# Row means from eight extra columns of a weight matrix, and reciprocal roots spread by two fp32r products, in the last stage of a four-layer kernel

## Chip, core and metric

One core of a Trainium2 chip runs the whole program in one launch. The metric is the device time of that launch in microseconds. TensorE (PE in the profile) multiplies, ScalarE (ACT) and VectorE (DVE) take tiles out of PSUM, GpSimd (POOL) works on SBUF alone, and SyncE (SP) issues nearly all transfers.

## What is computed

The input x is (8, 256, 256) fp32: 2048 tokens of 256 channels. Four residual layers follow each other, cut here to what matters:

```python
x = x + L0(x)      # 3 shared dense layers and 2 of 4 experts per batch, mixed by a gate
x = x + L1(x)      # 8 gated experts (silu(x Wg) * (x Wu)) Wd weighted per batch, and a shared one
def L2(x):         # per batch b a language id picks W1 (256x64), b1, W2 (64x256), b2, gamma, beta
    h = relu(x @ w1 + b1)
    x = x + (h @ w2 + b2)
    mean = x.mean(-1); var = ((x - mean) ** 2).mean(-1)
    return (x - mean) * rsqrt(var + 1e-5) * gamma + beta
x = x + L2(x)
def L3(x):         # per batch b a subject id picks weight (256x256) and bias
    return x @ weight.T + bias
x = x + L3(x)
```

## The kernel before

Channels lie on the partitions, in two halves of 128 (`dt` 0 and 1), and tokens along the free dimension. An fp32 product is made of three fp32r products: each operand is held as a rounded part (`xh`, made by ACT with a Copy) and the rest (`xl`, made by DVE or POOL as a difference), and `product` (L439) adds hi by hi, hi by lo and lo by hi.

**The last stage** works off the ninth expert of layer 1 in five jobs of tokens, `LAST_JOBS` (L39): three of 512 tokens and two of 256. Each job has eight steps T. In a step PE issues the twelve products of `last_up` (L760) for tile T and the six of `last_down` (L780) for tile T - 2; ACT makes the silu (L1387) and the rounded hidden tile (L1395), DVE multiplies (L2243) and takes the difference (L2250). So `last_up(n)` waits for DVE's product of tile n - 2 (`gated_done`), and `last_down(n)` for the difference of tile n (`hid_lo`).

**Layers 2 and 3** of a job ride on the steps of the jobs behind it. The five jobs are the units 0 to 4 of `unit` (L303); the last, 4, is called `END`. The table `WHEN` (L54) gives for each unit and each stage name the step T behind which the stage's instructions stand, on each engine in its own program order. For a unit i they are:

- `last_take` (L2224, DVE) adds job i into x; `x2` makes its parts (ACT L1412, DVE L2279). `xs` sums the two channel halves of x for units 1 and 2 (POOL L1848), and splits the sum (ACT L1455, POOL L1504).
- `up`: `l2_up_stage` (PE, L803), the first matrix of layer 2, 64 rows into PSUM. `mean`: `mean_stage` (PE, L831), products with `minus_mean`, a 128x128 tile filled with -1/256, which leave minus the row mean in every partition: two of 512 columns for units 1 and 2 (L841, L842), two per channel half and part, four in all, for units 0 and 3 (L850, L851). For END `mean_part` (L822) issues eight of 256 columns (L828), four ahead of `x_part(4, 0)` and four behind the wait for the hidden tile.
- `hid` (or `within` for unit 0, inside a step): ACT writes relu of the hidden tile twice, as fp32 and as fp32r (L1445, L1446), once per batch; DVE adds the mean to x (L2291, twice) and writes the difference of the hidden tile into the lower 64 rows of `u` (L2294).
- `down`: `l2_down_stage` (PE, L854), both parts of the second matrix against the 128 rows of `u`. END's `x_part(4, 1)` follows it.
- `res` (DVE, L2308), `square` (ACT L1421, DVE L2317, L2321, POOL L1859), `scale` (ACT, L1431), `var` (PE, L884), `eps` (DVE, L2328), then on POOL the power -1/2 (L1866) and on ACT `diag` (L1462), which scales the 128x128 unit matrix by the reciprocal root, a block of 128 tokens at a time.
- `rstd` (PE, L892): an fp32 product of ones with that diagonal matrix spreads the roots over all partitions. END has no `diag` and no `rstd`.
- `norm` (DVE, L2337), `add` (DVE, L2347), `x3` and `x3l` (ACT L1412, DVE L2279), `l3a` and `l3b` (PE, L908 to L910), `outa` and `outb` (DVE, L2395), and the store (SP, L431).

END ends otherwise: `split` (ACT L1476, DVE L2363), `scaled` (PE, L955 to L957), `base` (DVE, L2373) and `final` (DVE, L2383).

Weights of layers 2 and 3 are loaded late, one batch b per chunk: `w3_plus_one` and `late_lo` (POOL, L1822, L1831), `center_w2` (DVE, L2255) and `late_hi` (ACT, L1397), spread by `late_step` (L299). `b2_stage` (PE, L797) and `center_b2` (DVE, L2266) stand at T = 9.

## Time and profile before

| | us |
|---|---|
| median of 3 runs | 1579.68 |
| their lowest and highest | 1579.55, 1579.96 |
| the profiled execution's own time | 1579.32 |
| its span, first to last instruction | 1577.2 |
| busy share of the span: PE, PE's weight loads, DVE, ACT, POOL | 100%, 85%, 72%, 59%, 43% |
| mean granted clock of TensorE | 0.999 of full speed |

The span is the time between the first and the last instruction of one execution; 2.1 us of that execution lie around it. Starts are counted from the span's start. A row of the timeline gives start, duration, engine, line, operation, the tile written and the tiles read, shapes, a count where equal instructions are merged, and in brackets the idle time ahead of it with the instruction that ended it. Ends of matmuls are modelled: the distance from one start to the next tells more than a duration.

### The profile page before, as it was taken

How to read it: one execution, taken by the hardware profiler on the slowest of the kernel's cores; microseconds unless marked ns; L12 is line 12 of the kernel's file. 1: busy time of each engine (PE TensorE's matmuls, PEld its weight loads, DVE VectorE, ACT ScalarE, POOL GpSimd, SP SyncE). 2: the span in 40 equal slices, each digit the busy share in tenths (PEclk: the TensorE clock that was granted, in tenths of full speed). 3: DMA queues.
4: the chain of work that ended last, by engine and by line, in shares of the span. 5: the costliest groups of instructions: out<-in, count | busy, mean ns of one | idle time of the engine just before them, and what ended most of it. 6: DMA issues, size and time to landing. Idle time of an engine off the chain costs nothing.

```text
span 1577.2 us, 22436 instructions
## 1 busy us (share of the span) xinstructions
PE 1571.8 (100%) x7916; PEld 1341.1 (85%) x7916; DVE 1132.3 (72%) x1685; ACT 930.7 (59%) x1683; POOL 674.7 (43%) x631
## 2 busy tenths in 40 slices
PE   9999999999999999999999999999999999999999
PEld 7888888999988888888888888888888888888898
DVE  6855556688889876776777776776776776657567
ACT  6655555666666665565565566666656666555444
POOL 7865544756786441431432432342342352038000
PEclk9999999999999999999999999999999999999999
DMA  4111105455420000000010010010010010022000
GB/s 161 55 54 53 54 27 187 161 178 181 174 85 27 27 28 27 22 33 27 15 41 28 14 41 27 14 40 28 14 41 27 14 41 27 15 60 77 14 14 28
DMA packets 31013, 85.98 MB, mean 55 GB/s; under 512 B 5031, under 2 KB 10535, under 8 KB 30775
## 3 DMA queue, kind: packets, MB, share of 16 engines
q1 hardware_dynamic: 30310, 83.21, 15.5%
q8 instruction: 63, 1.03, 0.3%
q0 software_dynamic: 304, 1.10, 0.2%
q14 instruction: 48, 0.39, 0.1%
q10 hardware_dynamic: 288, 0.26, 0.1%
HBM read 82.46 MB, written 2.10 MB: 54 GB/s over the span
## 4 chain that ended last, share of the span: by engine, by line
PE 97%; issue 2%; POOL 1%; DMA 0%; ACT 0%; DVE 0%; POOLq 0%; DVEq 0%
PE up L684 13%; PE up L682 13%; PE up L683 13%; PE sum L441 13%; PE sum L443 13%; PE sum L442 13%; PE up L441 4%; PE up L442 4%; PE up L443 4%; PE up L449 2%; PE up L451 2%; PE up L450 2%; POOL expert_in L1504 0%; PE sum L630 0%; DMA raw<-in_shared 0%
## 5 line engine op out<-in xcount | busy, mean ns | idle before, releaser
L1313 ACT ACTIVATE hidden_hi<-up_tile 128x512 fp32r<-128x512 f32 x256 | 161.3, 630 | 189.3 <-DVE up_tile L2155 166.7
L2160 DVE TENSOR_TENSOR hidden_lo<-up_tile,hidden_hi 128x512 fp32r<-128x512 f32 x256 | 197.8, 792 | 44.7 <-ACT hidden_hi L1313 44.7
L2150 DVE TENSOR_TENSOR gate_tile<-up,gate_tile 128x512 f32<-128x512 f32 x192 | 129.9, 687 | 139.1 <-PE up L684 138.5
L443 PE MATMUL sum<-hidden_hi,down 128*128 128x512 f32 x512 | 199.2, 389 | 0.0
L441 PE MATMUL sum<-hidden_hi,down 128*128 128x512 f32 x512 | 199.2, 389 | 0.0
L442 PE MATMUL sum<-hidden_lo,down 128*128 128x512 f32 x512 | 199.2, 389 | 0.0
L684 PE MATMUL up<-x_sums,gate_up 128*128 128x512 f32 x512 | 199.2, 389 | 0.0
L682 PE MATMUL up<-x_sums,gate_up 128*128 128x512 f32 x512 | 199.2, 389 | 0.0
L683 PE MATMUL up<-x_sums,gate_up 128*128 128x512 f32 x512 | 199.2, 389 | 0.0
L2155 DVE TENSOR_TENSOR up_tile<-up_tile,gate_tile 128x512 f32<-128x512 f32 x192 | 183.8, 984 | 2.2
L1306 ACT ACTIVATE gate_tile<-gate_tile 128x512 f32<-128x512 f32 x192 | 119.8, 632 | 90.5 <-DVE gate_tile L2150 88.3
L1504 POOL TENSOR_TENSOR gate_up<-raw,gate_up 128x384 fp32r<-128x384 f32 x60 | 67.8, 1130 | 204.3 <-ACT gate_up L1257 204.3
L1302 ACT ACTIVATE gate_tile<-up 128x512 f32<-128x512 f32 x192 | 110.6, 594 | 68.0 <-PE up L684 64.4
L682 PE MATMUL up<-x_hi,gate_up 128*128 128x512 f32 x384 | 149.6, 390 | 0.0
L684 PE MATMUL up<-x_hi,gate_up 128*128 128x512 f32 x384 | 149.4, 389 | 0.0
L683 PE MATMUL up<-x_lo,gate_up 128*128 128x512 f32 x384 | 149.4, 389 | 0.0
L1504 POOL TENSOR_TENSOR expert_in<-raw,expert_in 128x256 fp32r<-128x256 f32 (+1 forms) x112 | 102.7, 934 | 78.0 <-ACT expert_in L1011 78.0
L2150 DVE TENSOR_TENSOR up_tile<-up,up_tile 128x512 f32<-128x512 f32 x192 | 130.1, 687 | 2.7 <-PE up L684 0.7
L1302 ACT ACTIVATE up_tile<-up 128x512 f32<-128x512 f32 x192 | 112.0, 600 | 21.3 <-PE up L684 15.6
L1648 POOL TENSOR_TENSOR weight_sums<-raw 128x256 f32<-128x256 f32 x30 | 28.9, 964 | 204.7 <-PE up L684 204.7
L441 PEld LDWEIGHTS sum<-hidden_hi,down 128*128 128x128 f32 x512 | 96.1, 188 | 20.7 <-DVE hidden_lo L2160 1.1
L682 PEld LDWEIGHTS up<-x_sums,gate_up 128*128 128x128 f32 x512 | 96.1, 188 | 20.2 <-ACT gate_tile L1302 0.2
(332 smaller groups left out, 4012.3 us busy)
## 6 DMA issues: line engine op xcount, KB each, us to landing
raw<-in_experts SPq DMA_DIRECT2D x64, 512.0 KB, 3.2
raw<-in_l SPq DMA_DIRECT2D x51, 512.0 KB, 3.2
raw<-in_shared SPq DMA_DIRECT2D x23, 512.0 KB, 3.2
raw<-in_w SPq DMA_DIRECT2D x8, 256.0 KB, 2.5
x<-in_xT SPq DMA_DIRECT2D x3, 512.0 KB, 9.2
l_stage<-in_l SPq DMA_DIRECT2D x3, 512.0 KB, 4.2
out<-out_stage SPq DMA_DIRECT2D x6, 256.0 KB, 2.2
gate_w<-in_gw POOLq DMA_DIRECT2D x1, 1024.0 KB, 6.3
```

The costliest lines, as they stand in the source:

```text
L441: pe.matmul(out, wh, vh, start=start, stop=False)
L442: pe.matmul(out, wh, vl, start=False, stop=False)
L443: return pe.matmul(out, wl, vh, start=False, stop=stop)
L682: pe.matmul(out, wh, vh, start=first, stop=False, skip_group_check=True)
L683: pe.matmul(out, wh, vl, start=False, stop=False, skip_group_check=True)
L684: return pe.matmul(out, wl, vh, start=False, stop=True, skip_group_check=True)
L1302: A(out, ps, ACT.Copy).then_inc(q_done[m], 1)
L1313: A(hi[:, i], cu[:, i], ACT.Copy).then_inc(hi_done, 1)
L1504: return nc.gpsimd.tensor_tensor(dst, src, hi.bitcast(f32), ALU.subtract)
L2150: V.tensor_tensor(t, ps, t, ALU.add).then_inc(c_done[m], 1)
L2155: V.tensor_tensor(cu[:, i], up, cg[:, RING[i]], ALU.mult).then_inc(gat_done, 1)
L2160: V.tensor_tensor(lo[:, i], cu[:, i], hi[:, i].bitcast(f32), ALU.subtract).then_inc(lo_done, 1)
```

## The change

Two things are replaced. **Row means**: the first matrix of layer 2 gets eight more columns (64 to 71) per batch and channel half, each filled with -1/256 in the rounded part and 0 in the rest, so that `up` also leaves minus the row mean of x in eight PSUM rows. DVE copies these rows into rows 64 to 71 of a new fp32r tile `v` and their rest into rows 96 to 103; the other lower rows of `v` are zeroed once. The lower 64 rows of the rest of the second matrix (`w2[b][64:128, 1]`) are filled with rows that are 1 at row 64 and at row 96 and 0 elsewhere, so that the product with `v` adds the mean. `mean_stage`, `mean_part`, `row_sum`, `row_sum_hi` and the sums L2291 go, and `res` reads x. ACT writes the fp32r relu into `u` and `v` with one instruction of twice the columns. **Roots**: for units 0 to 2 POOL rounds the roots (`rhi`) and takes the rest (`rlo`); ACT makes the diagonal matrix of the one, DVE that of the other, and PE spreads them with two fp32r products. Unit 3 stays as it was. Besides, `b2_stage` and `center_b2` move from T = 9 to T = 6, `late_hi(7)` behind `x2` of unit 0, and END's second `x_part` ahead of its `down`.

```diff
-                if "xs" in WHEN[i]:
-                    pe.wait_ge(xs_lo, i)
-                    pe.matmul(out, minus_mean[:], xsr[i // 2][:, 0, 0:n], start=True, stop=False)
-                    pe.matmul(out, minus_mean[:], xsr[i // 2][:, 1, 0:n], start=False, stop=True).then_inc(mean_done, 1)
-                    return
-                last = product_of_parts(out, t0, n)
-                last.then_inc(mean_done, 1)
...
-                        last = product(unit_ps[i][0:A2, 0, c], w1r[:, b, 0, m], w1r[:, b, 1, m],
+                        last = product(unit_ps[i][0:A2 + MEAN_ROWS, 0, c], w1m[:, b, 0, dt], w1m[:, b, 1, dt],
                                        xh[:, dt, t], xl[:, dt, t], dt == 0, dt == DT - 1)
...
                 if i == END:
                     pe.wait_ge(out_ready, 6)
-                    mean_part(i, 1)
                     x_part(i, 0)
+                    x_part(i, 1)
                 pe.wait_ge(hid_relu, i + 1)
-                if i == END:
-                    mean_part(i, 0)
-                else:
-                    pe.wait_ge(x_centered, i + 1)
                 pe.wait_ge(l2_hid, i + 1)
+                pe.wait_ge(picked, b0 + nb)
...
-                        last = pe.matmul(out, w2[b][:, 1, k], u[:, c], start=False, stop=True, skip_group_check=True)
+                        last = pe.matmul(out, w2[b][:, 1, k], v[:, c], start=False, stop=True)
                 last.then_inc(l2_down, 1)
-                if i == END:
-                    x_part(i, 1)
...
                 pe.wait_ge(diag_done, i + 1)
-                pe.matmul(unit_ps[i][:, 1, c0:c0 + n], ones[:],
-                          diag[:, c0 // P:(c0 + n) // P].rearrange("p q n -> p (q n)"),
-                          start=True, stop=True).then_inc(rstd_bc, 1)
+                if i == 0:
+                    pe.wait_ge(ones_done, 1)
+                if i < SUMMED:
+                    pe.matmul(unit_ps[i][:, 1], ones_r[:], diag[:].rearrange("p q n -> p (q n)"), start=True, stop=False)
+                    pe.wait_ge(diag_lo_done, i + 1)
+                    pe.matmul(unit_ps[i][:, 1], ones_r[:], diag_lo[:].rearrange("p q n -> p (q n)"),
+                              start=False, stop=True).then_inc(rstd_bc, 1)
...
-            hooks.setdefault(9, []).insert(0, b2_stage)
+            hooks.setdefault(6, []).insert(0, b2_stage)
...
+                if b < 2:
+                    pick_rows(b)
                 A(w2[b][:, 0], raw[:, s, 640:896], ACT.Copy).then_inc(w_hi, 1)
+
+            def pick_rows(b):
+
+                A(w2[b][A2:2 * A2, 1], pick[A2:2 * A2].to_broadcast([A2, D]), ACT.Copy).then_inc(picked, 1)
...
-                    last = A(u[0:A2, c], unit_ps[i][0:A2, 0, c], ACT.Relu, bias=b1[:, b:b + 1])
+                    twice = unit_ps[i][0:A2, 0, c].rearrange("p (o n) -> p o n", o=1).to_broadcast([A2, 2, S])
+                    last = A(uv[0:A2, :, c], twice, ACT.Relu, bias=b1[:, b:b + 1])
                 last.then_inc(hid_relu, 1)
...
+            hooks[late_step(B - 1)].append(hooks[late_step(B - 1)].pop(0))
+            for b in range(2, B):
+                hooks.setdefault((10, 18, 19)[b // 2 - 1], []).append(lambda b=b: pick_rows(b))
...
                 G(rstd[:, q], var[:, q], mhalf[:, q], ALU.pow).then_inc(rstd_done, 1)
+                if i < SUMMED:
+                    pool.wait_ge(rstd_done, i + 1)
+                    G(rhi[:], rstd[:], ones[:, 0:4], ALU.mult).then_inc(rstd_hi, 1)
+                    pool.wait_ge(rstd_hi, i + 1)
+                    G(rlo[:], rstd[:], rhi[:].bitcast(f32), ALU.subtract).then_inc(rstd_lo, 1)
...
+            def mean_columns(h):
+
+                same = ones[:].rearrange("p (b t m) -> p b t m", b=B, t=DT)
+                V.tensor_scalar(w1m[:, :, h, :, A2:A2 + MEAN_ROWS], same, (-1.0 / D, 0.0)[h], None, ALU.mult)
+
+            def zero_rows():
+
+                dve.wait_ge(w_lo, PLAIN0 + L1_CH * NE1 + B)
+                linked(V.tensor_scalar(v[A2:2 * A2], ones[A2:2 * A2, 0:1].to_broadcast([A2, BLK]), 0.0, None, ALU.mult))
...
-                if i != END:
-                    dve.wait_ge(mean_done, i + 1)
-                    if i:
-                        dve.wait_ge(x3_done, DT * i)
-                    for dt in range(DT):
-                        last = V.tensor_tensor(y[:, dt, c], x[:, dt, t0:t0 + n], unit_ps[i][:, 1, c], ALU.add)
-                    last.then_inc(x_centered, 1)
+                dve.wait_ge(l2_up, i + 1)
+                if i:
+                    dve.wait_ge(l2_down, i)
+                m, r = slice(A2, A2 + MEAN_ROWS), slice(A2 + 32, A2 + 32 + MEAN_ROWS)
+                linked(V.tensor_copy(v[m, c], unit_ps[i][m, 0, c]))
+                V.tensor_tensor(v[r, c], unit_ps[i][m, 0, c], v[m, c].bitcast(f32), ALU.subtract)
                 dve.wait_ge(hid_relu, i + 1)
                 V.tensor_tensor(u[A2:2 * A2, c], ru[:, c], u[0:A2, c].bitcast(f32), ALU.subtract).then_inc(l2_hid, 1)
...
+            def diag_lo_stage(i):
+
+                if i >= SUMMED:
+                    return
+                dve.wait_ge(rstd_lo, i + 1)
+                V.tensor_tensor(diag_lo[:], ident[:].rearrange("p (o n) -> p o n", o=1).to_broadcast([P, 4, P]),
+                                rlo[:].rearrange("p (q o) -> p q o", o=1).to_broadcast([P, 4, P]),
+                                ALU.mult).then_inc(diag_lo_done, 1)
...
+                            "hid": hid_stage, "res": res_stage, "square": square_stage, "eps": eps_stage, "diag": diag_lo_stage,
...
+            hooks.setdefault(10, []).append(whole_ones)
+            hooks.setdefault(6, []).append(center_b2)
+            hooks.setdefault(10, []).append(zero_rows)
+            for h in range(2):
+                hooks.setdefault(4 + h, []).append(lambda h=h: mean_columns(h))
```

## Rows read from the trace of the kernel before

**Rows 1.** The page: the chain that ended last, by engine.

```profile
PE 97%; issue 2%; POOL 1%; DMA 0%; ACT 0%; DVE 0%; POOLq 0%; DVEq 0%
```

**Rows 2.** Window of the last stage: stretch, length, busy (count) of PE, PEld, DVE, ACT, POOL, clock.

```profile
1530.00:1540.00 10.00, 10.00 (x84) 9.91 (x83) 7.59 (x17) 4.64 (x12) 0.00 (x0) 1.00 0.06 19
```

**Rows 3.** Timeline of PE: the four mean products of unit 0, to the product behind them.

```profile
1454.02 0.40 PE L850 MATMUL sum<-x_hi,minus_mean 128*128 128x512 f32 x1
...
1454.96 0.40 PE L441 MATMUL up<-x_hi,last_gate_up 128*128 128x512 f32 x1
```

**Rows 4.** Timeline of PE: unit 1's fp32 spreading product, and the next two blocks' starts.

```profile
1509.41 1.02 PE L892 MATMUL sum<-rstd_diag,ones 128*128 128x512 f32 x2
...
1513.01 0.39 PE L441 MATMUL sum<-hidden_hi,last_down 128*128 128x512 f32 x1
...
1514.37 0.28 PE L441 MATMUL up<-x_hi,last_gate_up 128*128 128x256 f32 x1
```

**Rows 5.** Timelines around T = 10 and 11: POOL's last weights, a DVE step, a PE step.

```profile
1446.70 6.31 POOL L1504 TENSOR_TENSOR l_w<-raw,l_w 128x512 fp32r<-128x512 f32 x6
...
1455.30 0.68 DVE L2243 TENSOR_TENSOR up_tile<-up,gate_tile 128x512 f32<-128x512 f32 x1
...
1460.01 0.40 PE L441 MATMUL up<-x_hi,last_gate_up 128*128 128x512 f32 x1
```

**Rows 6.** Lines of POOL in the whole trace: count, ns min/median/max, first and last start.

```profile
L1828 POOL TENSOR_TENSOR raw<-raw,ident x16: 452/462/922, 1420.4 to 1446.3; 128x128 f32<-128x128 f32 x16
...
L1504 POOL TENSOR_TENSOR down<-raw,down x30: 1284/1293/1619, 483.9 to 1322.3; 128x512 fp32r<-128x512 f32 x30
...
L1859 POOL TENSOR_TENSOR squares<-y x2: 612/612/613, 1558.3 to 1570.6; 128x256 f32<-128x256 f32 x2
...
L1866 POOL TENSOR_TENSOR rstd<-variance,minus_half x5: 695/1017/1027, 1466.0 to 1573.2; 128x4 f32<-128x4 f32 x3, 128x2 f32<-128x2 f32 x2
```

**Rows 7.** Timelines, unit 1: from the diagonal matrix to the first product of layer 3.

```profile
1507.21 1.28 ACT L1462 ACTIVATE rstd_diag<-ident,rstd 128x128 f32<-128x128 f32 x4 [0.33 <-POOL rstd L1866]
...
1509.01 0.69 DVE L2243 TENSOR_TENSOR up_tile<-up,gate_tile 128x512 f32<-128x512 f32 x1 [2.92 <-ACT gate_tile L1387]
...
1515.90 1.29 DVE L2279 TENSOR_TENSOR x_lo<-x,x_hi 128x512 fp32r<-128x512 f32 x2
...
1517.19 0.28 PE L908 MATMUL sum<-l_w,x_hi 128*128 128x256 f32 x1
```

**Rows 8.** Groups by line and form, 1400 us to the end: count, busy us, mean ns, idle before.

```profile
L1395 ACT ACTIVATE hidden_hi<-up_tile 128x512 fp32r<-128x512 f32 x24 | 15.2, 632 | 27.3 <-DVE up_tile L2243 17.5 <-PE sum L443 9.7
...
L1395 ACT ACTIVATE hidden_hi<-up_tile 128x256 fp32r<-128x256 f32 x16 | 6.7, 418 | 17.6 <-DVE up_tile L2243 17.6
...
L2291 DVE TENSOR_TENSOR y<-x,sum 128x512 f32<-128x512 f32 x6 | 3.8, 680 | 0.4 <-PE sum L842 0.4
```

**Rows 9.** Timelines, units 2 and 3: ACT, then DVE, up to the first product of unit 3.

```profile
1534.98 0.38 ACT L1387 ACTIVATE gate_tile<-up 128x256 f32<-128x256 f32 x1 [0.20 <-PE up L443]
...
1544.03 0.88 DVE L2232 SCALAR_TENSOR_TENSOR x<-sum,l_coef,x 128x256 f32<-128x256 f32 x2 [0.17 <-PE sum L443]
...
1544.88 0.42 DVE L2243 TENSOR_TENSOR up_tile<-up,gate_tile 128x256 f32<-128x256 f32 x1
...
1548.58 0.75 DVE L2279 TENSOR_TENSOR x_lo<-x,x_hi 128x256 fp32r<-128x256 f32 x2
...
1549.13 0.30 PE L441 MATMUL up<-x_hi,l_w 128*64 128x256 f32 x1
```

**Rows 10.** Timelines of the tail: END's hidden tile, its second matrix, squares and variance.

```profile
1568.75 0.42 DVE L2294 TENSOR_TENSOR l_hidden_r<-l_hidden,l_hidden_r 64x256 fp32r<-64x256 f32 x1 [0.66 <-ACT l_hidden_r L1446]
...
1569.35 0.28 PE L871 MATMUL sum<-l_hidden_r,l_w 128*128 128x256 f32 x1
...
1570.93 0.55 DVE L2317 TENSOR_TENSOR squares<-y 128x256 f32<-128x256 f32 x1
...
1571.97 0.95 PE L884 MATMUL sum<-ones,squares 128*128 128x1 f32 x8
```

More of the change, by code:

```diff
@@ L21 @@
 FT = F // P
+MEAN_ROWS = 8
 NB = 4
@@ L49 @@
 RING = [0, 1, 2, 0]
-STAGES = ["x2", "xs", "up", "mean", "within", "hid", "down", "res", "square", "scale", "var", "eps", "diag", "rstd",
+STAGES = ["x2", "up", "within", "hid", "down", "res", "square", "scale", "var", "eps", "diag", "rstd",
           "norm", "add", "x3", "x3l", "l3a", "outa", "l3b", "outb"]
 WHEN = [dict(zip(STAGES, at)) for at in (
[4 rows of a table removed]
-for u in (0, 3):
-    del WHEN[u]["xs"]
[4 rows of a table added]
 for u in (1, 2, 3):
@@ L122, in build @@
     ones = place("ones", [P, P], f32)
+    ones_r = place("ones_r", [P, P], f32r)
+    rhi, rlo = place("rstd_hi", [P, 4], f32r), place("rstd_lo", [P, 4], f32)
     types = place("types", [P, B], i32)
@@ L155, in build @@
     ws = [place(f"weight_sums{s}", [P, 2, 7 * P], f32, over=f"gate_up{s}", skip=7 * K1) for s in range(PAIRS)]
-    xst = place("x_row_sum", [P, BLK], f32, over="raw", skip=14336)
-    xsr = [place(f"x_row_sum_parts{r}", [P, 2, BLK], f32r, over="weights", skip=(12 - 4 * r) * K1) for r in range(2)]
     cg = place("gate_tile", [P, 3, BLK], f32, over="weights", skip=88 * K1)
@@ L182, in build @@
     biasb = place("l3_bias", [P, B, D], f32, over="shared_sums")
-    diag = place("rstd_diag", [P, 4, P], f32, over="shared_sums", skip=4 * B * D)
+    diag = place("rstd_diag", [P, 4, P], f32r, over="shared_sums", skip=4 * B * D)
     ident = place("ident", [P, P], f32, over="shared_sums", skip=4 * B * D + 16 * P)
@@ L820, in l2_up_stage, with l2_down_stage @@
                 last.then_inc(l2_up, 1)
-            def mean_part(i, m):
+            def l2_down_stage(i):
                 b0, nb, t0, c0, n = unit(i)
-                out = unit_ps[i][:, m, c0:c0 + n]
-                for dt in range(DT):
-                    for part in (xh, xl):
-                        pe.matmul(out, minus_mean[:], part[:, dt, t0:t0 + n], start=dt == 0 and part is xh, stop=False,
-                                  skip_group_check=True)
-            def mean_stage(i):
-                b0, nb, t0, c0, n = unit(i)
-                out = unit_ps[i][:, 1, c0:c0 + n]
-                if i == 0:
-                    pe.wait_ge(b2_done, 1)
@@ L847, in product_of_parts @@
-            def product_of_parts(out, t0, n):
-                for dt in range(DT):
-                    pe.matmul(out, minus_mean[:], xh[:, dt, t0:t0 + n], start=dt == 0, stop=False)
-                    last = pe.matmul(out, minus_mean[:], xl[:, dt, t0:t0 + n], start=False, stop=dt == DT - 1)
-                return last
-            def l2_down_stage(i):
-                b0, nb, t0, c0, n = unit(i)
                 if i == END:
                     pe.wait_ge(out_ready, 6)
-                    mean_part(i, 1)
@@ L870, in l2_down_stage @@
                         out, k = unit_ps[i][:, m, c], slice(m * P, (m + 1) * P)
-                        pe.matmul(out, w2[b][:, 0, k], u[:, c], start=i != END, stop=False, skip_group_check=True)
-                        last = pe.matmul(out, w2[b][:, 1, k], u[:, c], start=False, stop=True, skip_group_check=True)
+                        pe.matmul(out, w2[b][:, 0, k], u[:, c], start=True, stop=False)
+                        last = pe.matmul(out, w2[b][:, 1, k], v[:, c], start=False, stop=True)
                 last.then_inc(l2_down, 1)
-                if i == END:
-                    x_part(i, 1)
             def var_stage(i):
@@ L2259, in center_w2 @@
                 w = raw[:, s, 640:896]
+                if b == 0:
+                    dve.wait_ge(ident_full, 16)
+                    V.tensor_tensor(pick[:], ident[:, A2:A2 + 1], ident[:, A2 + 32:A2 + 33], ALU.add)
                 if b:
@@ L2266, in center_b2 @@
             def center_b2():
-                V.tensor_scalar(minus_mean[:], ones[:], -1.0 / D, None, ALU.mult)
                 dve.wait_ge(b2_sum, 1)
```

78 lines of the change are left out of this document (35 added, 43 removed), and 8 rows, old and new, of the table WHEN.

## The prediction

> **What bounds the kernel now.** I read the page first: the chain that ended last is 97% PE [rows 1]. So a product that goes is worth its whole issue time, unless another engine's chain sets when PE may go on. I then read the last stage, where all edits lie, by windows: PE is full at a granted clock of 1.00, while DVE is busy for three quarters [rows 2]. The reader should see that DVE has spare time on average, and none where a chain of DVE and ACT ends just as PE needs it. For those places I compared, in the timelines, the end of what a PE instruction waits for with its start.
>
> **Mean products.** Four products of 512 columns take 1454.96 - 1454.02 = 0.94 us for unit 0 [rows 3], 0.235 apiece. Units 1 and 2 have two wide ones each, 0.47 us. Ten microseconds hold 84 products, nearly all of 256 columns [rows 2], so such a one takes 0.12, and unit 3's four 0.48. END's eight narrow ones are worth 8 x 0.12 = 0.96 us at most. The 72 columns in place of 64 in the first matrix cost nothing: products are paid by their moving columns, and weight loads run beside them. The second matrix keeps its count.
>
> **Spreading products.** Six wide fp32r products of `last_down` take 1514.37 - 1513.01 = 1.36 us, 0.227 apiece. The fp32 one of unit 1 starts at 1509.41, and between it and 1513.01 lie the twelve of `last_up`, 2.72 us, so it took 3.60 - 2.72 = 0.88 us [rows 4]. Two fp32r ones take 0.45. Each of units 0 to 2 can save 0.43 us.
>
> PE issue time removed is thus 0.94 + 0.47 + 0.47 + 0.48 + 0.96 + 3 x 0.43 = 4.6 us. What follows is how much of it the other engines let through.
>
> **Preparation.** At T = 4 and 5 DVE fills the mean columns, at T = 6 it centres b2 instead of at T = 9, at T = 10 it copies the ones and zeroes 64 rows of 512 (0.3 and at most 0.7 us, taking L2291's 680 ns for a 512-column DVE instruction [rows 8]). The zeroing waits for POOL's last weights, which ended at 1446.70 + 6.31 = 1453.0 us and may end some 0.6 later with `late_hi(7)` behind `x2`. Queued behind that wait is DVE's product at 1455.30; the PE step that needs it is the one starting at 1460.01, or 0.94 earlier after the change [rows 5]. Cover is 3 us, so I put it at nothing; without that cover it would be about 1 us once. ACT's eight row fills of 64x256 (at most 0.42 us each, by L1395's 256 columns [rows 8]) stand where it otherwise waits for PE. POOL loses two row sums, ACT two splits. The transfers don't change. The first matrix of unit 0 still starts where PE comes to it.
>
> **Hidden tile.** ACT writes 512 columns instead of 256: 632 - 418 = 0.21 us more per batch [rows 8], 0.43 per wide unit. DVE trades two sums of 680 ns for a copy and a difference of the same 512 columns, on eight partitions; I take the same time each, as time goes by columns. For units 0 and 1 this ends well ahead of `down`. **For unit 3** the one longer relu stands straight ahead of DVE's difference and of `down`; I keep back about half of its 0.21, so the means give 0.48 - 0.12 = 0.36 us.
>
> **The roots, units 0 and 1.** POOL gets two instructions of 4 columns between the power and the others. None that short is in the trace except the power, 1.02 us. Addition and subtraction go by columns, 452 ns at 128 and 1284 at 512 at the least [rows 6]: 2.17 ns a column, which leaves 0.18 us at 4 columns. Bounds are 0.1 and 1.02; I take 0.2, plus 0.06 for the hand-over, nearest to the like operation. So ACT's diagonal starts 0.26 late. ACT's diagonal ended at 1507.21 + 1.28 = 1508.49, 0.92 ahead of PE's product [rows 4, 7], so the product itself doesn't wait. DVE's own diagonal (0.7 us) fits while it waits for ACT: it idled 2.92 us ahead of its next product [rows 7]. But from ACT's diagonal on everything is back to back: silu, product, rounding, norm, add, up to the parts of x that `l3a` needs. In unit 1 the second half was ready at 1515.90 + 1.29 = 1517.19, and PE began at 1517.19 and needed it three products of 0.12 later: a margin of 0.30 us with the hand-over [rows 7]. PE comes 0.43 earlier and the parts 0.26 later: a stall of 0.39. Unit 1's root thus nets 0.04 us; unit 0 has over a microsecond of margin there and keeps 0.43.
>
> **Units 2 and 3, where most is lost.** At T = 30 ACT's silu waited only 0.20 us for PE [rows 9]; ACT's longer relu pushes the chain ahead of it 0.21 back, so PE's gain of 0.47 there doesn't speed this chain. It runs through residual, squares, and three steps of product and rounding to the parts of unit 3, and PE's first matrix of unit 3 started at 1549.13, just behind the first half of them (1548.58 + 0.4) [rows 9]: margin none. DVE's new diagonal stands right behind the take at 1544.03, and the product of 1544.88 comes 0.60 later. The take itself can come 0.17 earlier, since it waited that long for PE [rows 9]. So the first matrix of unit 3 starts 0.60 - 0.17 = about 0.4 us later than before, although PE arrives 0.47 + 0.43 = 0.90 earlier; all that is lost as a new stall of 1.2 to 1.3 us there.
>
> **Tail.** END's `down` started at 1569.35, right behind the mean products, with DVE's difference ending at 1568.75 + 0.42 = 1569.17 [rows 10]. After: ACT's relu is 0.21 longer and DVE's copy and difference (2 x 0.42) stand ahead, so `down` starts about 0.15 later, now waiting for DVE. But the second `x_part` is already done, so the variance waits for DVE's square instead of PE: 1570.93 + 0.55 + 0.15 + 0.05 = 1571.68 against 1571.97 [rows 10]. Gain 0.27 of the 0.96. POOL, DVE and the store behind are unchanged.
>
> **Sum**, against the profiled execution (1579.32, of which the span is 1577.2): -0.94 - 0.43 (unit 0), -0.47 - 0.04 (unit 1), +0.40 (units 2 and 3 up to the first matrix), -0.36 (unit 3), -0.27 (tail) = -2.1 us, so 1577.2. The median of the runs shown is 0.36 higher, so I forecast 1577.6.
>
> **Rivals.** (a) **The cover holds**: the chains of units 1 to 3 are shorter than I read, and only the tail keeps back something. Then 0.94 + 0.43 + 0.47 + 0.43 + 0.47 + 0.43 + 0.48 + 0.27 = 3.9 us go: 1575.8. For it speaks DVE's idle time in every step; against it the zero margin at 1549.13.
>
> (b) **GpSimd's short instructions are as long as its wide ones**, 1.28 us [rows 6]. DVE then waits at its diagonal of T = 13 and T = 21 for three of them in a row, and the next product, ACT's rounding and x's parts wait behind it. In unit 1's times, the power's end at 1507.2, two of 1.28 with hand-overs, DVE's 0.7 and PE's 0.23 end at 1510.95, where the fp32 product ended at 1510.29 [rows 4, 7]; so unit 0's root costs about +0.7 where it saved 0.43. DVE's next product comes 1.6 late, against the margin of 0.30, so unit 1's root costs +1.3. In unit 2 the diagonal starts 0.9 later than in the forecast: 0.4 + 0.9 = +1.3. In all -0.94 + 0.7 - 0.47 + 1.3 + 1.3 - 0.36 - 0.27 = +1.3: 1581.0, slower than before. At 1.02 apiece the same sum gives -0.94 + 0.2 - 0.47 + 0.75 + 0.7 - 0.36 - 0.27 = -0.4, so it decides from about 1.1 us. For it speaks the power's 1.02 us at 4 columns; against it that the power's shortest, at 2 columns, is 0.70 [rows 6], so its time lies in its columns.
>
> (c) **A first-use stall on GpSimd**: its first multiplication stands idle for microseconds in unit 0 and PE with it. In the trace the multiplication of POOL ran 612 and 613 ns, first and second alike [rows 6], so I give it little. Were it as long as POOL's last run of late weights, 6.3 us [rows 5], less PE's margin of 0.9: 1577.6 + 5.4 = 1583.0. The Trainium skill, GPSIMD Engine Reference, "Instruction dispatch", says that the first call to a freshly loaded kernel pays about 6 us that no instruction shows. Nothing in the trace shows it, and the equal pair speaks against it.
>
> That the change does not do what it says is ruled out for PE: the products are gone from the program.
>
> **Numbers.** A measurement here tells about 0.2% (3.2 us) from no change, so faster means below 1576.5. Forecast 70%, 1576.4 to 1578.8; (a) 23%; (b) 4%; (c) 3%. The range takes in (a) and the bounds of the short instructions: 1575.4 to 1579.0. Faster: nearly all of (a), little of the forecast, 24%; slower by over 0.2%: (c) and the worse end of (b), 4%; same 72%.
>
> **What would show it.** PE's 20 mean products missing; the spreading pair 0.45 us long; no gap of PE before T = 24; a gap of about 0.4 us ahead of `l3a` of unit 1 and of over 1 us ahead of the first matrix of unit 3; POOL's new pair under 0.3 us each; END's `down` waiting for DVE. If the gap at unit 3 is missing, (a) is right; if DVE stands more than 3 us at T = 13, (b) or (c).

## The result, and the profile after

The changed kernel takes 1581.81 us (median of 22 runs, 1579.67 to 1585.13), the kernel before beside it 1579.97 (22 runs, 1577.56 to 1582.14). The ratio is 1.0012, with a 95% interval of 1.0006 to 1.0017: about 1.9 us slower. The forecast was 1577.6, its range ended at 1579.0. The profiled execution took 1581.88, with a span of 1579.8.

The chain of the page has lost PE's near-monopoly, against [rows 1]:

```profile
PE 92%; DVE 3%; issue 2%; ACT 1%; POOL 1%; DMA 0%; POOLq 0%; ACTq 0%; DVEq 0%
```

To find where, I cut the last stage at three PE instructions that both kernels have: the first product of the stage, the first of unit 0's first matrix of layer 2, and the first of unit 0's variance. These are the timeline rows of PE; first the kernel before, then the changed one.

```profile
1402.08 0.39 PE L441 MATMUL up<-x_hi,last_gate_up 128*128 128x512 f32 x1
...
1452.64 0.28 PE L441 MATMUL sum<-x_hi,l_w 128*64 128x256 f32 x1
...
1464.11 0.16 PE L884 MATMUL sum<-ones,squares 128*128 128x1 f32 x1
```

```profile
1402.64 0.39 PE L443 MATMUL up<-x_hi,last_gate_up 128*128 128x512 f32 x1
...
1455.10 0.31 PE L443 MATMUL sum<-x_hi,l_w_mean 128*72 128x256 f32 x1 [1.13 <-DVE x_lo L2270]
...
1467.36 0.27 PE L851 MATMUL sum<-ones,squares 128*128 128x1 f32 x1 [0.59 <-DVE squares L2308]
```

From the first to the third it is 62.03 us before and 64.72 after: **2.69 us lost** where I had expected 0.94 gained. I call this the first stretch. From the variance to the end of the span it is 1577.2 - 1464.11 = 113.09 against 1579.8 - 1467.36 = 112.44: 0.65 gained, the second stretch. Together +2.04 us, which is the measured difference. What lies ahead of the stage's first product scatters by several us from one execution to the next, whatever the kernel, so I compare stretches rather than single times from here on. One kernel was profiled twice (cols_b9 and b9_timed below): its two stretches came out within 0.01 us of each other.

Busy time by windows tells which engine changed. The columns are the stretch, its length, busy time (count) of PE, PEld, DVE, ACT and POOL, the clock, DMA share and GB/s. Before, then after:

```profile
1400.00:1440.00 40.00, 40.00 (x178) 33.10 (x178) 24.29 (x38) 20.43 (x40) 27.57 (x32) 1.00 0.42 116
1440.00:1470.00 30.00, 30.00 (x147) 24.92 (x145) 20.60 (x36) 16.33 (x37) 12.40 (x16) 1.00 0.03 8
```

```profile
1400.00:1440.00 40.00, 40.00 (x179) 33.16 (x178) 27.04 (x40) 19.87 (x38) 24.35 (x29) 1.00 0.39 105
1440.00:1470.00 30.00, 27.77 (x131) 21.73 (x131) 24.70 (x37) 16.73 (x38) 14.84 (x19) 1.00 0.09 23
```

The clock is full in both. DVE has two instructions more in the first window and one more in the second, yet is busy 2.75 and 4.10 us longer: the instructions themselves are longer. The groups of DVE by line and form from 1400 to 1466 us (busy us, mean ns) say which, before and then after:

```profile
L2243 DVE TENSOR_TENSOR up_tile<-up,gate_tile 128x512 f32<-128x512 f32 x14 | 9.6, 687 | 9.3 <-ACT gate_tile L1387 9.3
L2263 DVE SCALAR_TENSOR_TENSOR raw<-w_sum,raw 128x256 f32<-128x256 f32 x8 | 5.8, 731 | 0.3
L2262 DVE TENSOR_REDUCE w_sum<-raw 128x1 f32<-128x256 f32 x8 | 3.3, 409 | 0.1
L2279 DVE TENSOR_TENSOR x_lo<-x,x_hi 128x512 fp32r<-128x512 f32 x2 | 2.5, 1310 | 0.7 <-ACT x_hi L1412 0.7
```

```profile
L2218 DVE TENSOR_TENSOR up_tile<-up,gate_tile 128x512 f32<-128x512 f32 x13 | 8.9, 685 | 7.2 <-ACT gate_tile L1361 7.0
L2241 DVE SCALAR_TENSOR_TENSOR raw<-w_sum,raw 128x256 f32<-128x256 f32 x8 | 8.4, 1054 | 0.3
L2240 DVE TENSOR_REDUCE w_sum<-raw 128x1 f32<-128x256 f32 x8 | 3.3, 410 | 0.5 <-DVE raw L2241 0.5
L2270 DVE TENSOR_TENSOR x_lo<-x,x_hi 128x512 fp32r<-128x512 f32 x2 | 3.7, 1906 | 0.0
L2254 DVE TENSOR_SCALAR l_w_mean<-ones 128x128 fp32r<-128x128 f32 x2 | 1.8, 894 | 0.0
```

The product that reads PSUM and the reduction are as long as ever. The centring of the second matrices (L2263, now L2241) and the rest of x, which read two SBUF tensors, went from 5.8 to 8.4 and from 2.5 to 3.7 us for the same work. What they run beside is in the timelines of DVE and POOL of the changed kernel:

```profile
1417.77 0.15 DVE L2237 TENSOR_TENSOR pick_rows<-ident 128x1 f32<-128x1 f32 x1
...
1418.25 2.72 POOL L1486 TENSOR_TENSOR last_down<-raw,last_down 128x512 fp32r<-128x512 f32 x2 [2.61 <-ACT last_down L1260]
...
1418.29 1.54 DVE L2241 SCALAR_TENSOR_TENSOR raw<-w_sum,raw 128x256 f32<-128x256 f32 x1
...
1427.79 1.27 POOL L1486 TENSOR_TENSOR l_w<-raw,l_w 128x512 fp32r<-128x512 f32 x1
...
1427.87 2.60 DVE L2241 SCALAR_TENSOR_TENSOR raw<-w_sum,raw 128x256 f32<-128x256 f32 x1
...
1429.03 0.46 POOL L1486 TENSOR_TENSOR l_w_mean<-raw,l_w_mean 128x128 fp32r<-128x128 f32 x1
...
1429.46 0.73 POOL L1486 TENSOR_TENSOR l_w<-raw,l_w 64x256 fp32r<-64x256 f32 x1
...
1430.15 1.05 POOL L1810 TENSOR_TENSOR raw<-raw,ident 128x128 f32<-128x128 f32 x2
```

and of the kernel before at the first of these places:

```profile
1417.66 0.42 DVE L2263 SCALAR_TENSOR_TENSOR raw<-w_sum,raw 128x256 f32<-128x256 f32 x1
...
1417.69 2.79 POOL L1504 TENSOR_TENSOR last_down<-raw,last_down 128x512 fp32r<-128x512 f32 x2 [2.61 <-ACT last_down L1286]
```

Started 0.03 us ahead of GpSimd's instruction the centring takes 0.42 us; started 0.04 behind it, 1.54. At 1427.87 it stays past two ends of GpSimd's instructions and takes 2.60. The Trainium skill, GPSIMD Engine Reference, "Specifications", says that GpSimd shares its SBUF interfaces with VectorE, to the cost of VectorE instructions with two SBUF inputs or in a 2-port mode, and the Trainium skill, SBUF — State Buffer, "SBUF: two separate sides", that whichever of the two starts first keeps the pair for its whole instruction. By the first, the trace agrees, reduction and PSUM operand included. By the second, it agrees at 1418.29: the row's two POOL instructions take 2.72, so the first ends near 1419.5 and the centring at 1419.83. At 1427.87 it would have been DVE's turn at 1429.03, and DVE ended at 1430.47: there the measurement decides, and it goes beyond the page.

**Theory**: the preparation that I put at nothing shifts and lengthens DVE's sequence at T = 2 to 9, its instructions fall behind GpSimd's, and from T = 10 to 13 PE waits for DVE (its blocks of products are at their usual length up to 1443.7 us, T = 9). **Rivals**: ACT's row fills cost by themselves; the new place of `late_hi(7)`; the split roots; or DVE is merely short of time and GpSimd plays no part.

### The profile page after: what moved, and what is told of

Same layout as the page of the kernel before. It is cut to its first block, busy times and chain, and to the rows that moved or that the text cites. A ratio compares the mean times of both kernels' runs of the same rounds, so it can differ in the third digit from the quotient of the medians.

```text
span 1579.8 us, 22414 instructions
## 1 busy us (share of the span) xinstructions
PE 1570.2 (99%) x7896; PEld 1338.1 (85%) x7896; DVE 1141.8 (72%) x1694; ACT 934.0 (59%) x1689; POOL 670.4 (42%) x633
## 4 chain that ended last, share of the span: by engine, by line
PE 92%; DVE 3%; issue 2%; ACT 1%; POOL 1%; DMA 0%; POOLq 0%; ACTq 0%; DVEq 0%
PE up L685 13%; PE up L684 13%; PE up L686 13%; PE sum L443 12%; PE sum L444 12%; PE sum L445 12%; PE up L443 3%; PE up L444 3%; PE up L445 3%; PE up L452 2%; PE up L451 2%; PE up L453 2%; DVE up_tile L2218 1%; ACT hidden_hi L1369 0%; DVE raw L2241 0%
```

## The experiments

Stretches of every kernel, in us, by the same three PE rows and the end of the span (my subtraction). Each row is one profiled execution:

| kernel | to unit 0's first matrix | first stretch | second stretch | both |
|---|---|---|---|---|
| before | 50.56 | 62.03 | 113.09 | 175.12 |
| changed | 52.46 | 64.72 | 112.44 | 177.16 |
| before_fills | 50.59 | 62.09 | 113.20 | 175.29 |
| hi7_back | 52.48 | 64.74 | 112.37 | 177.11 |
| roots_back | 52.45 | 64.72 | 112.37 | 177.09 |
| picks_late | 52.25 | 63.48 | 112.35 | 175.83 |
| before_tiny | 50.57 | 62.04 | 113.06 | 175.10 |
| pick_moved | 50.57 | 63.73 | 112.23 | 175.96 |
| cols_act_only | 50.66 | 63.78 | 112.30 | 176.08 |
| cols_on_act | 51.36 | 62.59 | 112.18 | 174.77 |
| cols_act_hi7 | 51.39 | 63.75 | 112.35 | 176.10 |
| cols_hi7_roots2 | 51.35 | 63.74 | 111.96 | 175.70 |
| cols_norest | 51.36 | 62.44 | 112.34 | 174.78 |
| cols_b9 | 50.57 | 61.57 | 112.29 | 173.86 |
| b9_only | 53.76 | 65.92 | 112.29 | 178.21 |
| b9_late | 51.80 | 63.01 | 112.39 | 175.40 |
| b9_timed | 50.57 | 61.58 | 112.28 | 173.86 |
| b9_roots2 | 50.57 | 61.57 | 112.05 | 173.62 |

### One part at a time

**picks_late**: the row fills of the first two batches at T = 10.

```diff
-                if b < 2:
-                    pick_rows(b)
...
-            for b in range(2, B):
-                hooks.setdefault((10, 18, 19)[b // 2 - 1], []).append(lambda b=b: pick_rows(b))
+            for b in range(B):
+                hooks.setdefault((10, 10, 18, 19)[b // 2], []).append(lambda b=b: pick_rows(b))
```

> The changed kernel with the row fills of batches 0 and 1 moved out of late_hi to T = 10. First stretch (first product of T = 0 to the variance of unit 0): 62.0 us before the change, 64.7 after. Theory (the two fills hold POOL back, and POOL's runs then fall on DVE's instructions with two SBUF inputs): the first stretch falls by 2 us or more, DVE's L2241 of T = 4 is no longer 2.6 us long, and the whole time falls by about as much. Rival (late_hi(7) behind x2 is the cause) and rival (the mean columns on DVE at T = 4 and 5): the first stretch stays within 0.4 us of 64.7.

**hi7_back**: `late_hi(7)` ahead of `x2` again.

```diff
-            hooks[late_step(B - 1)].append(hooks[late_step(B - 1)].pop(0))
```

> The changed kernel with late_hi(7) back ahead of x2 of unit 0. Rival (moving it put POOL's last two weights into one run over the x_lo pair, 3.73 us for two instructions against 2.54 before): the pair falls to 2.6 us or less and the first stretch by 1 us or more. Theory (the fills of T = 3 and 4): x_hi comes 0.9 us later, the pair may shorten, and the first stretch stays at 64.7 within 0.5.

**roots_back**: the fp32 spreading product for units 0 to 2 again, without `rhi`, `rlo` and DVE's diagonal (SPLIT is 0).

```diff
-                if i < SUMMED:
+                if SPLIT <= i < SUMMED:
+                    pe.matmul(unit_ps[i][:, 1], ones[:], diag_wide[:].rearrange("p q n -> p (q n)"),
+                              start=True, stop=True).then_inc(rstd_bc, 1)
+                elif i < SPLIT:
...
```

> The changed kernel with the fp32 spreading product in units 0 to 2 and neither rhi, rlo nor DVE's diagonal. By my account of the chains the roots pay 0.43 us in unit 0 and 0.04 in unit 1 and cost 0.6 ahead of unit 3's first matrix: the second stretch (variance of unit 0 to the end, 112.4 us after) changes by -0.4 to +0.2 and the stall of 1.0 us ahead of unit 3's first matrix goes. Rival (the roots are what made the change slower): the whole falls by 1.5 us or more. The first stretch stays at 64.7.

**before_fills**: the kernel before, with two ACT copies into a spare tile where the change fills rows (extra work that nothing reads).

```diff
                 act.wait_ge(w2_centered, b + 1)
+                if b < 2:
+                    A(spare[A2:2 * A2], ones[A2:2 * A2, 0:1].to_broadcast([A2, D]), ACT.Copy)
...
```

> The kernel before with two ACT copies of 64x256 into a spare tile, where the changed kernel fills its rows in late_hi of batches 0 and 1: 0.8 us of work on an engine that waits there, and nothing else. Theory: POOL starts later, its phase against DVE moves, and the first stretch (62.0 us) grows by 1 us or more. Rivals: it grows by less than 0.3 us.

Time against the kernel before, twelve executions each: picks_late 1.0004 (0.9995 to 1.0013), hi7_back 1.0013 (1.0004 to 1.0022), roots_back 1.0007 (0.9999 to 1.0016), before_fills 1.0001 (0.9992 to 1.0010). These intervals overlap; the stretches are sharper. Neither `late_hi(7)` nor the roots have to do with the loss here (64.74 and 64.72, and the two rests of x still take 3.71 us with `late_hi(7)` back). Fills alone cost the kernel before nothing (62.09), against what I expected; with them late the centring of T = 4 takes 1.49 us and not 2.60, and the changed kernel's first stretch is 1.24 shorter, less than the 2 us expected and more than the rivals' 0.4. So the fills hurt only in company, and 1.45 us over the kernel before stay. The roots are also worth nothing in sum: against roots_back the changed kernel gains 0.32 us from the variance to unit 1's first matrix and 0.07 from there to unit 2's, and loses 0.36 from there to unit 3's.

### DVE's part

**before_tiny**: the kernel before, with a one-column DVE sum into a spare tile at T = 2. **pick_moved**: picks_late, with `pick` taken from T = 2 to T = 6. **cols_on_act**: pick_moved, with the mean columns filled by ACT at T = 1. **cols_act_only**: the changed kernel with that last edit alone.

```diff
+                if b == 0:
+                    dve.wait_ge(ident_full, 16)
+                    V.tensor_tensor(spare[:], ident[:, A2:A2 + 1], ident[:, A2 + 32:A2 + 33], ALU.add)
```

```diff
-                if b == 0:
-                    dve.wait_ge(ident_full, 16)
-                    V.tensor_tensor(pick[:], ident[:, A2:A2 + 1], ident[:, A2 + 32:A2 + 33], ALU.add)
...
             def center_b2():
+                V.tensor_tensor(pick[:], ident[:, A2:A2 + 1], ident[:, A2 + 32:A2 + 33], ALU.add)
```

```diff
-            for h in range(2):
-                hooks.setdefault(4 + h, []).append(lambda h=h: mean_columns(h))
...
-            hooks[1] = [lambda: last_gate_up_hi(3)]
+            hooks[1] = [lambda: last_gate_up_hi(3), mean_columns]
...
+                for h in range(2):
+                    A(w1m[:, :, h, :, A2:A2 + MEAN_ROWS], same, ACT.Copy, scale=(-1.0 / D, 0.0)[h])
```

> The kernel before with one more DVE sum of one column (128x1, into a spare tile that nothing reads) at T = 2, ahead of the first centring. Theory (order of starts on DVE and GpSimd decides): the first centring takes 1.54 us in place of 0.42, and the stretch to unit 0's variance is 62.1 to 62.6 us in place of 62.03; all of it if what comes behind has no room, nothing if it has. Rival (it costs its own 0.15 us at most): first centring 0.42 to 0.66 us, stretch 62.0 to 62.2.

> As the kernel of the late row fills, with DVE's one-column sum `pick` (0.15 us) taken from T = 2, ahead of the first centring of the second matrices, to T = 6. Stretch from the first product of the last stage to unit 0's variance: 62.03 us in the kernel before, 64.72 after the change, 63.48 with the late fills. Theory (DVE's instructions with two SBUF inputs are held while GpSimd runs, and the 0.15 us push the first centring behind a GpSimd start): that centring takes 0.42 us in place of 1.54 and the stretch shortens by 0.3 to 1.1 us against 63.48. Rival (so short an instruction changes nothing that is felt): 63.4 to 63.5. Second stretch, variance of unit 0 to the end: 112.4 by both.

> As the kernel with the late fills and the moved pick, with the mean columns filled by ACT at T = 1 in place of DVE at T = 4 and 5. Theory (DVE is short of time at T = 4 to 10, since its instructions are held): the stretch to unit 0's variance falls by the two fills (0.48 and 1.31 us) and what they push behind GpSimd, to 61.1 to 62.0 us. Rival (DVE has cover there, and the loss lies in the zeroing of rows or the earlier b2 centring): no more than 0.2 us less than the kernel with the moved pick. Second stretch 112.4 by both.

> The changed kernel with the mean columns on ACT at T = 1 alone; fills and pick as in the change. Theory (the two mean-column instructions on DVE cost about half of the loss): stretch to unit 0's variance 62.9 to 63.9 us in place of 64.72. Rival (the row fills on ACT are the whole of what can be had): 64.6 to 64.8. Second stretch 112.4 by both.

Timelines of DVE and POOL at T = 2, of before_tiny:

```profile
1419.53 0.15 DVE L2263 TENSOR_TENSOR spare<-ident 128x1 f32<-128x1 f32 x1
...
1420.05 1.53 DVE L2267 SCALAR_TENSOR_TENSOR raw<-w_sum,raw 128x256 f32<-128x256 f32 x1
...
1420.01 2.72 POOL L1505 TENSOR_TENSOR last_down<-raw,last_down 128x512 fp32r<-128x512 f32 x2 [2.60 <-ACT last_down L1287]
```

and of pick_moved:

```profile
1416.52 0.42 DVE L2236 SCALAR_TENSOR_TENSOR raw<-w_sum,raw 128x256 f32<-128x256 f32 x1
...
1416.55 2.79 POOL L1484 TENSOR_TENSOR last_down<-raw,last_down 128x512 fp32r<-128x512 f32 x2 [2.60 <-ACT last_down L1260]
```

**That the order of the two starts decides is shown both ways**: a one-column sum of 0.15 us, which moves the next centring by 0.07, makes it 1.1 us longer, and taking it away gives them back. But before_tiny's first stretch is 62.04: in the kernel before, DVE's idle time takes the 1.1 us in. One hold costs nothing; it needs a sequence without room. No run took GpSimd's own work away, so what the holds cost in sum isn't measured by itself.

pick_moved came out within neither expectation: PE reaches unit 0's first matrix at 50.57, as early as before, and then loses it again (63.73); the rest of x takes 3.35 us there, where it took 1.29 in picks_late. At its new place `pick`, the sum of one column, is itself held: 1.25 us for 0.15. cols_on_act met the theory only in part: 62.59, where 61.1 to 62.0 was expected, and 63.5 by the rival. cols_act_only is in the theory's range with 63.78. Taking DVE's two fills away is worth about 1 us in either company.

### The rest of the preparation

**cols_act_hi7**: cols_on_act with `late_hi(7)` back. **cols_hi7_roots2**: that, with the fp32 product for unit 2 alone. **cols_norest**: cols_on_act, without the rounding rest of unit 0's means (one DVE difference left out). **cols_b9**: cols_on_act with b2's two steps back at T = 9.

```diff
-                V.tensor_tensor(v[r, c], unit_ps[i][m, 0, c], v[m, c].bitcast(f32), ALU.subtract)
+                if i:
+                    V.tensor_tensor(v[r, c], unit_ps[i][m, 0, c], v[m, c].bitcast(f32), ALU.subtract)
```

```diff
-            hooks.setdefault(6, []).insert(0, b2_stage)
+            hooks.setdefault(9, []).insert(0, b2_stage)
...
-            hooks.setdefault(6, []).append(center_b2)
+            hooks.setdefault(9, []).append(center_b2)
```

> The kernel with late fills, moved pick and the mean columns on ACT, and the last batch's split `late_hi(7)` back ahead of `x2`. With it behind `x2`, the kernel with the columns on ACT had 51.36 us from the first product of the last stage to the first matrix of unit 0 (50.56 in the kernel before), with one wait of PE of 0.65 us at T = 9, where a centring of DVE was held to 1.87 us by GpSimd. Theory (GpSimd's place decides what is held): with `late_hi(7)` as in the kernel before, the split of x that GpSimd overlaps is longer (2.5 us) but the wait at T = 9 goes: 50.5 to 50.8 us to the first matrix, 61.8 to 62.0 to unit 0's variance. Rival (the place of `late_hi(7)` is of no account, as it was in the changed kernel): 51.3 to 51.4 and 62.5 to 62.6. Second stretch 112.2.

> The same with unit 2's root spread by one fp32 product as in the kernel before (units 0 and 1 keep the two fp32r ones). First stretch as in that kernel. Second stretch: by the chain that I read (DVE's second diagonal of T = 32 stands ahead of the chain that ends at unit 3's first matrix) the distance from unit 2's first matrix to unit 3's is 21.9 us in place of 22.2 to 22.3, and variance of unit 0 to the end 111.8 to 112.0 in place of 112.2 to 112.4. Rival (PE's 0.43 us count there as anywhere): 22.6 and 112.6.

> The kernel with the columns on ACT, without unit 0's DVE difference that keeps the rounding rest of the row means (0.69 us of DVE; the rest stays zero for unit 0, all else is computed). In that kernel PE stood 0.65 us ahead of unit 0's variance, waiting for DVE's squares. Theory (from the first matrix of unit 0 on, DVE's instructions follow each other without room, so DVE sets when the variance starts, and of the 0.94 us that PE's mean products took only the margin of 0.3 us can be had): the distance from the first matrix to the variance is 10.6 us in place of 11.23. Rival (ACT or PE sets it): 11.2.

> The kernel with the columns on ACT, with b2's product and its centring back at T = 9, where they were in the kernel before. Theory: the centring of b2 at T = 6 is not what loses time; the stretch to unit 0's first matrix is 51.0 to 51.6 us (51.36 with it at T = 6) unless the new order of DVE and GpSimd starts holds another pair. Rival (DVE at T = 6 to 8 is where the time goes): 50.6.

cols_act_hi7 went against the theory: PE's wait for the chain behind the centring that is held at T = 9 stayed (51.39; PE stands ahead of its products of T = 11), and the rest of x, 2.23 us instead of 1.29, costs 1.1 us behind it. In this company the place that the change gave `late_hi(7)` is the better one. cols_hi7_roots2 confirmed the reading of unit 2: 111.96 in place of 112.35.

cols_norest was expected at 10.6 us between first matrix and variance by the theory and measured 11.08, from 11.23. With 0.69 us of DVE gone only 0.15 came out, and its DVE row shows who took over:

```profile
1458.09 0.69 DVE L2283 TENSOR_TENSOR l_hidden_r<-l_hidden,l_hidden_r 64x512 fp32r<-64x512 f32 x1 [0.59 <-ACT l_hidden_r L1432]
```

So DVE and ACT's relus end within 0.2 us of each other there; DVE alone does not set it. cols_b9 gave 50.57 and 61.57, in all 173.86, and its stretches are the first to beat those of the kernel before by more than 1 us. That is the rival's 50.6 and not my 51.0 to 51.6: in this company b2's centring at T = 6 was what lost the last 0.8 us. It ran again as b9_timed, below.

**b9_only**: the changed kernel with only b2's steps back at T = 9. **b9_late**: that and the late fills. **b9_roots2**: cols_b9 with the fp32 product for unit 2 (SPLIT is 2). **b9_timed**: cols_b9 again.

> The changed kernel with b2's product and centring back at T = 9 and nothing else (fills of the first two batches, pick and mean columns as in the change). Stretch from the first product of the last stage to the first matrix of unit 0: 50.56 us in the kernel before, 52.46 in the changed one; to unit 0's variance 62.03 and 64.72. Theory 1 (DVE's sequence at T = 4 to 8 is what loses, each part its share, b2's centring about 0.8 of it, as between the two kernels with the columns on ACT): 51.5 to 51.8 to the first matrix, 63.6 to 64.0 to the variance. Theory 2 (b2's move is the whole of it): 50.6 and 61.6. Rival (the other parts put the same instructions behind GpSimd again): 52.2 or more, 64.5 or more.

> The changed kernel with b2 back at T = 9 and the fills of the first two batches at T = 10 (the kernel with late fills alone had 52.25 and 63.48 us; pick and mean columns stay with DVE as in the change). Theory 1 (shares): 51.4 and 62.6. Theory 2 (b2's move is the whole): 50.6 and 61.6. Rival: as with late fills alone.

> Late fills, moved pick, mean columns on ACT, b2 at T = 9, and one fp32 spreading product for unit 2 as in the kernel before. From the stretches of its parts: first stretch 61.57 us, second 112.0, in all 173.5 to 173.6 where the kernel before has 175.12 and the changed one 177.16. Theory (what lies ahead of the last stage is the same program and takes the same time on average): 1.5 us under the kernel before, ratio 0.9990, and 3.6 under the changed one. Rival (the stretches differ by what one execution happened to have): ratio 0.9998 to 1.0005.

> The same without the last part (unit 2's root spread by two fp32r products as in the change). First stretch 61.57 us, second 112.3, in all 173.9: 1.2 us under the kernel before, ratio 0.9992; by the rival 0.9998 to 1.0005.

b9_only is the surprise: 65.92, **1.2 us worse than the change**, where by shares it should have been 0.9 better. In its timeline of DVE, ahead of PE's first matrix of unit 0 at 1457.85 (which waits for b2), stand two held instructions:

```profile
1452.04 1.94 DVE L2225 TENSOR_TENSOR hidden_lo<-up_tile,hidden_hi 128x512 fp32r<-128x512 f32 x1 [0.70 <-ACT hidden_hi L1369]
1453.90 3.31 DVE L2270 TENSOR_TENSOR x_lo<-x,x_hi 128x512 fp32r<-128x512 f32 x2
```

PE stood 2.05 us there, and then its granted clock fell to 0.50, the lower of its two levels, which it did in no other profile between 1400 and 1574 us. A window row of this kernel, columns as above:

```profile
1460.00:1462.00 2.00, 2.00 (x7) 1.52 (x6) 1.79 (x4) 1.98 (x5) 0.00 (x0) 0.50 0.00 0
```

Its products between 1458.5 and 1462.2 take up to 0.43 us apiece in place of 0.23. So only the way to the first matrix can be put down to DVE without the clock: 53.76 for 52.46, 1.3 us worse. From there to the variance it is 12.16 us for 12.26, with slow products in the place of waits.

The same edit that costs 1.2 us here gains 1.0 in cols_on_act (to the first matrix: 1.3 lost, 0.8 gained), and with the late fills alone, b9_late, it gains 0.5 (63.01 for 63.48), less than by shares (62.6) or if b2 were the whole (61.6). The parts don't add, so no share of the loss belongs to any one of them. What can be said is that with fills late, `pick` moved, columns on ACT and b2 at T = 9 the loss is gone. b9_roots2 measured 173.62, as expected from its parts (173.5 to 173.6), and over eleven executions a ratio of **0.9982 (0.9973 to 0.9991)**, 1578.27 us against 1581.67: faster than the kernel before, and by the two ratios faster than the changed one, which was not timed beside it. Its stretches explain 1.5 us. The medians differ by 3.4, the ratio says 2.8 (1.4 to 4.3 by its interval); whether the rest is more than scatter stays open. b9_timed gave 0.9992 (0.9983 to 1.0001), where 0.9992 was expected.

PE's waits from 1438 us on, of the changed kernel (us in total, times, longest) and of b9_roots2:

```profile
PE sum L443 <- DVE x_lo L2270: 1.4, 2, 1.1
PE up L443 <- DVE x_lo L2270: 1.0, 1, 1.0
PE sum L851 <- DVE squares L2308: 0.6, 1, 0.6
...
```

```profile
PE up L445 <- DVE x_lo L2275: 0.4, 1, 0.4
...
PE sum L853 <- DVE squares L2313: 0.3, 1, 0.3
...
```

## Why the prediction was wrong

**Preparation, put at nothing: this is the step that failed.** "Cover is 3 us, so I put it at nothing; without that cover it would be about 1 us once", and "The first matrix of unit 0 still starts where PE comes to it". I had looked for cover at the last link, T = 10 and 11 [rows 5], and priced the zeroing and ACT's fills by columns; DVE's own fills, `pick` and b2's earlier centring got no price. The zeroing was 0.42 us, within the 0.7 allowed. **The preparation cost 3.1 us in the place of nothing**: 64.72 us in the first stretch, against 61.58 in b9_timed, where it is spread otherwise. The loss was not at the link that I had priced, and only in part in the added instructions: DVE's fills at T = 4 and 5 took 0.48 and 1.31 us, b2's centring 1.07 where it had taken 0.18, and the unchanged centrings and rest of x 3.8 us more by the groups above. DVE's steps from T = 2 on feed each other through ACT and GpSimd, and from the end of T = 9 to unit 0's variance PE's blocks take 3.6 us more in all than their products. No rival of mine had it. (b) and (c) looked for GpSimd as the engine waited for; here it is the engine that holds another one up.

The warning stood in the trace of the kernel before: the eight equal centrings took from 0.42 to 1.49 us there, and unit 0's rest of x 2.54 for what takes 1.29 in unit 1 [rows 7], the time that I had quoted.

```profile
1438.34 1.49 DVE L2263 SCALAR_TENSOR_TENSOR raw<-w_sum,raw 128x256 f32<-128x256 f32 x1
...
1449.87 2.54 DVE L2279 TENSOR_TENSOR x_lo<-x,x_hi 128x512 fp32r<-128x512 f32 x2 [0.73 <-ACT x_hi L1412]
```

The last row also shows how thin the cover was at the links ahead of mine. It ended at 1452.41, and PE wanted its second half for the fourth product of the first matrix, 0.12 apiece from 1452.64 on: 0.6 us of margin. DVE's product of tile 10, which stands behind it, ended at 1453.30 + 0.68 = 1453.98, and PE's products of T = 12, which need it, began at 1454.96 [rows 3]; without the mean products ahead of them they begin 0.94 earlier, which leaves 0.04.

**Unit 0's mean, -0.94: half of it at best.** In the kernel before DVE's squares ended at 1463.07 + 0.69 = 1463.76, and PE took the variance at 1464.11:

```profile
1463.07 0.69 DVE L2321 TENSOR_TENSOR squares<-squares 128x512 f32<-128x512 f32 x1
```

A margin of 0.35, which I had not looked up for this unit. With the preparation out of the way the first stretch is 61.57, so 0.46 is what the mean gives; PE then stands 0.3 us for the squares, as the waits above show. I had also kept no part for the longer relu here, and cols_norest shows that it is as near as DVE.

**Unit 0's root, -0.43.** The spreading block and the twelve products behind it took 3.22 us against 3.60: 0.38. From the variance to unit 1's first matrix it is 0.27, since the variance's own block takes 0.92 us behind a wait, and 0.81 before.

**The short GpSimd instructions, 0.2 us**, and no first-use stall: right. Groups of POOL by line, after (the rounding, L1839, took as long, 200 ns):

```profile
L1841 POOL TENSOR_TENSOR rstd_lo<-rstd,rstd_hi 128x4 f32<-128x4 f32 x3 | 0.6, 201 | 0.2
```

Rivals (b) and (c) are out by these times.

**Unit 1, -0.51 with a stall of 0.39 at `l3a`: right.** From unit 1's first matrix to unit 2's it is 33.33 us in place of 33.85, 0.52 less. The timeline of PE, for [rows 4, 7]: the pair is 0.46 long, and the first four products of `l3a` start within 0.57 us (1519.34 to 1519.91) where three distances of 0.12 are usual.

```profile
1511.94 0.39 PE L862 MATMUL sum<-rstd_diag,ones_r 128*128 128x512 f32 x1
...
1512.17 0.39 PE L864 MATMUL sum<-rstd_diag_lo,ones_r 128*128 128x512 f32 x1
...
1519.34 0.36 PE L882 MATMUL sum<-l_w,x_hi 128*128 128x256 f32 x1
...
1519.91 0.39 PE L882 MATMUL sum<-l_w,x_hi 128*128 128x256 f32 x1
```

Its twelve products take 1.74 us, the next such block 1.43: a stall of 0.31 for the 0.39 forecast.

**Units 2 and 3 up to the first matrix, +0.40: right, measured +0.35** (22.28 against 21.93), for the reason given. For [rows 9]:

```profile
1547.10 0.68 DVE L2322 TENSOR_TENSOR rstd_diag_lo<-ident,rstd_lo 128x512 fp32r<-128x512 f32 x1
...
1551.38 0.75 DVE L2270 TENSOR_TENSOR x_lo<-x,x_hi 128x256 fp32r<-128x256 f32 x2
...
1551.94 0.31 PE L443 MATMUL up<-x_hi,l_w_mean 128*72 128x256 f32 x1 [1.04 <-DVE x_lo L2270]
```

PE stands 1.04 us there; I had said 1.2 to 1.3. With the fp32 product for unit 2 the wait is 0.4 and the distance 21.94, which shows DVE's diagonal as the cause.

**Unit 3, -0.36: measured -0.16.** Between its first matrix and the tail's first product of layer 3 lie 16.09 us against 16.25. The 0.48 of mean products is gone, but `down`, the root and the blocks ahead of them are 0.3 us longer: I kept back 0.12 for the longer relu, and that was too little.

**Tail, -0.27: measured -0.05.** `down` started behind DVE, as said, and the variance behind DVE's squares. For [rows 10]:

```profile
1571.58 0.42 DVE L2284 TENSOR_TENSOR l_hidden_r<-l_hidden,l_hidden_r 64x256 fp32r<-64x256 f32 x1
...
1572.10 0.36 PE L840 MATMUL sum<-l_hidden_r,l_w 128*128 128x256 f32 x1 [0.20 <-issue]
...
1574.45 1.02 PE L851 MATMUL sum<-ones,squares 128*128 128x1 f32 x8 [0.21 <-DVE squares L2304]
```

From the product of layer 3 on (1565.38 and 1568.03) the variance comes 0.17 earlier (the prediction's own sum, 1571.97 - 1571.68, is 0.29 and not 0.27), but from it to the end it is 5.35 us in place of 5.23.

The second stretch thus gave 0.65 of 1.17 us, with every sign right. The miss is the first: +2.69 for -0.94. And the first of my signs for a wrong forecast, "no gap of PE before T = 24", was the one that failed.

## What to carry to other kernels

Before an instruction is added to DVE, even one of 0.15 us, look at how equal DVE instructions differ in length around it: where the same form takes 0.4 us in one place and 1.5 in another, GpSimd is holding it, cover counted from the short ones isn't there, and each edit has to be read in company, not priced alone. Fills that depend on nothing belong on an engine and at a step that feeds no chain (here ACT at T = 1). And a product taken from PE is worth the smallest margin of any chain up to PE's next wait, which has to be read for every unit, not for the last ones alone.

## What the runs showed of the hardware

- The same DVE instruction (128x256, scalar-tensor-tensor in SBUF) took 0.42 to 3.73 us, by what GpSimd ran beside it. Reductions of the same size stayed at 0.41, and products with a PSUM operand at 0.68.
- A fill with one SBUF operand was held too: the same 128x128 instruction took 0.48 and 1.31 us, and a sum of one column 0.15 and 1.25.
- The longest centring, in cols_act_only, lasted from 1436.51 to 1440.24 across five ends of GpSimd instructions. At which of these DVE gets in differs for the same code: picks_late's centring of T = 4 took 1.49 us where the changed kernel's took 2.60, begun 0.09 and 0.08 us behind GpSimd's. I haven't found what decides it.
- The holding goes both ways: GpSimd's 128x128 subtraction took 0.46 us while DVE was held, and 0.65 where DVE came in between (changed kernel at 1442.48, picks_late at 1428.40).
- PE stood 1.1 us ahead of unit 0's first matrix in the changed kernel and kept a granted clock of 1.00; in b9_only it stood 2.05 there, and the clock was 0.50 from 1460 to 1462 us, 1.00 again from 1464 on.
